# A fused cross-attention kernel: where the low half of one split is subtracted

## The reference, cut to what matters

```python
# layer 0, by sample; 8 heads of 32 channels
q, k, v = Wq @ y + bq, Wk @ y + bk, Wv @ x + bv
attn = softmax(q_h @ k_h.T / sqrt(256))            # 32 x 32 a head
o = Wo @ (attn @ v) + bo + x
x1 = groupnorm(o) * gn_w + gn_b                    # over the whole sample
# layer 1, by chunk of 64 positions
q, k, v = proj(y)                                  # W_in, b_in
p = softmax(q_h @ k_h.T / sqrt(32) + mask)         # 64 x 64 a head and chunk
z = (W_out @ (p @ v) + b_out) * mask + x1
out = (z - mean(z)) * rsqrt(var(z) + eps)          # each channel, over positions
```

## Time and profile before

| | |
|---|---|
| median of three runs | 1559.06 us |
| the profiled execution | 1557.83 us |
| its span, first to last instruction | 1556.0 us |
| TensorE (PE) busy | 1527.3 us, 98% |
| VectorE (DVE) busy | 1324.1 us, 85% |
| ScalarE (ACT) busy | 999.5 us, 64% |
| GpSimd (POOL) busy | 451.4 us, 29% |
| mean granted TensorE clock | 0.996 |
| DMA, mean | 101 GB/s |
| VectorE, low half of `y` (line 820) | 64 instructions, 77.8 us |

### The profile page before, as it was taken

How to read it: one execution, slowest core, us unless ns; L and a number is a source line. 1 busy time by engine, 2 the same in 40 slices (tenths; PEclk the granted TensorE clock), 3 DMA queues, 4 the chain that set the end, 5 groups by cost and what they waited for, 6 DMA issues and landing times.

```text
span 1556.0 us, 55525 instructions
## 1 busy us (share of the span) xinstructions
PE 1527.3 (98%) x24660; PEld 1287.2 (83%) x24660; DVE 1324.1 (85%) x2028; ACT 999.5 (64%) x1808; POOL 451.4 (29%) x294
## 2 busy tenths in 40 slices
PE   9999999999999999999999999999999999999995
PEld 7888888888888888888888888888888888888874
DVE  5778888888898888988888888888888889898897
ACT  5656665666656667566575665766666665666655
POOL 1114133141331414214142241423314133141331
PEclk9999999999999999999999999999999999999998
DMA  7132331424324242241433415234142331424221
GB/s 256 54 96 77 110 123 41 145 84 117 110 67 133 70 142 86 83 123 63 143 83 103 124 45 151 88 98 123 49 150 79 120 111 55 133 82 127 59 72 67
DMA packets 96399, 157.33 MB, mean 101 GB/s; under 512 B 5408, under 2 KB 38304, under 8 KB 96032
## 3 DMA queue, kind: packets, MB, share of 16 engines
q1 hardware_dynamic: 96160, 153.78, 32.0%
HBM read 120.20 MB, written 33.55 MB: 99 GB/s over the span
## 4 chain that ended last, share of the span: by engine, by line
PE 86%; DVE 12%; issue 1%; ACT 1%; POOL 0%; ACTq 0%; POOLq 0%; DVEq 0%
PE pj_ps L313 41%; PE l_ps L313 12%; PE l_ps L433 7%; PE s_ps L337 7%; PE w_ps L348 7%; PE w_ps L366 6%; DVE o_sb L994 3%; PE s_ps L326 2%; PE l_ps L450 2%; DVE row_sum L851 1%; DVE prob L846 1%; DVE x_lo L829 1%; DVE y_lo L820 1%; DVE u_sb L868 1%; DVE m_lo L907 1%
## 5 line engine op out<-in xcount | busy, mean ns | idle before, releaser
L1125 POOL TENSOR_TENSOR prob<-prob,row_inv 128x1024 f32<-128x1024 f32 x128 | 258.3, 2018 | 903.8 <-DVE row_inv L856 903.8
L668 ACT CAST att_hi<-w_ps 128x256 fp32r<-128x256 f32 x256 | 82.9, 376 | 227.4 <-PE w_ps L366 221.0
L313 PE MATMUL pj_ps<-y_hi,w_hi 128*128 128x512 f32 x510 | 206.8, 405 | 0.0
L313 PE MATMUL pj_ps<-y_hi,w_lo 128*128 128x512 f32 x510 | 201.3, 395 | 0.0
L313 PE MATMUL pj_ps<-y_lo,w_hi 128*128 128x512 f32 x510 | 201.2, 394 | 0.0
L851 DVE TENSOR_REDUCE row_sum<-prob 128x16 f32<-128x1024 f32 x128 | 154.9, 1210 | 52.1 <-ACT prob L650 52.1
L839 DVE TENSOR_REDUCE row_max<-s_ps 128x16 f32<-128x1024 f32 x128 | 155.9, 1218 | 33.7 <-PE s_ps L337 31.1
L645 ACT COPY prob_t<-w_ps 128x512 f32<-128x512 f32 x256 | 149.8, 586 | 14.2 <-PE w_ps L348 11.4
L1142 POOL TENSOR_TENSOR o_sb<-o_sb,u_sb 128x1024 f32<-128x1024 f32 x60 | 157.9, 2642 | 2.6 <-ACT o_sb L658 2.6
L824 DVE TENSOR_TENSOR yt_hl<-yt_raw,yt_hl 128x1024 fp32r<-128x1024 f32 x64 | 119.8, 1872 | 42.7 <-ACT yt_hl L613 40.8
L846 DVE TENSOR_TENSOR prob<-s_ps,row_max 128x1024 f32<-128x1024 f32 x128 | 155.4, 1214 | 0.1
(11 more groups left out here) (141 smaller groups left out, 3540.0 us busy)
## 6 DMA issues: line engine op xcount, KB each, us to landing
y_raw<-in_ctx SPq DMA_DIRECT2D x64, 512.0 KB, 4.8
yt_raw<-in_ctx_t SPq DMA_DIRECT2D x64, 512.0 KB, 4.8
x_raw<-in_x SPq DMA_DIRECT2D x64, 512.0 KB, 5.3
out_z<-o_sb SPq DMA_DIRECT2D x60, 512.0 KB, 3.6
mask_b<-in_mask SPq DMA_DIRECT2D x64, 256.0 KB, 4.0
out_z<-o_sb SPq DMA_DIRECT2D x8, 256.0 KB, 2.6
u_sb<-in_w SPq DMA_DIRECT2D x2, 512.0 KB, 5.8
w_sb<-in_w SPq DMA_DIRECT2D x1, 1024.0 KB, 11.1
```

Of the source, the lines that this page charges most:

```text
L313: last = mm(dst, lhs, rhs, start=i == 0, stop=i == len(todo) - 1)
L1125: nc.gpsimd.tensor_tensor(cut, cut, row_inv[:, u % 2, :].unsqueeze(2).to_broadcast([P, 2 * HEADS, CHUNK]), ALU.mult).then_inc(probs_done, 1)
```

## The change

VectorE's call of `split_y` in the loop is removed (its two calls ahead of the loop stay). GpSimd gets a function of the same name with the same wait, operands and semaphore, called in the slots with j = 2, after the slot's `scale_probs`, `group_norm` and `join`. Before its loop GpSimd waits until the two low halves made ahead of it are counted. 62 subtractions move.

```diff
@@ VectorE, body of the loop
-                    if j == 2 and not (last and b + 2 >= BLOCKS):
-                        split_y(n, b + 2)
@@ GpSimd
+            def split_y(n, b):
+                pool.wait_ge(y_hi_done, count(n, 4, b))
+                nc.gpsimd.tensor_tensor(y_lo[:, b % 2], y_raw[:, b % 2], y_hi[:, b % 2], ALU.subtract).then_inc(y_lo_done, 1)
@@ GpSimd, body of the loop
                     if not first and T_Z <= s < T_Z + BLOCKS:
                         join(n - 1, s - T_Z)
+                    if s % PAIRS == 2 and not (last and s // PAIRS + 2 >= BLOCKS):
+                        split_y(n, s // PAIRS + 2)
                     if s == T_STAT and not first:
                         instance_norm(n - 1)
 
             pool.wait_ge(power_set, 1)
+            pool.wait_ge(y_lo_done, 2)
             over_samples(pool, body)
```

## The result

The changed kernel takes 1563.66 us in the median of 13 runs (1562.61 to 1564.56), the kernel before 1559.65 in 13 runs beside it: a ratio of 1.0025, with a 95% interval of 1.0016 to 1.0033, so 2.5 to 5.1 us slower. 1565.0 was forecast. The profiled execution took 1563.65 us, its span is 1561.9.

The account below looks back on a forecast made before the run. TensorE, busy 1527.3 of 1556.0 us, was taken as the bound. A loss of 12.6 us at a_wide less 6.7 won at o_bias gives +5.9, put on the median of 1559.06: 1565.0 us, range 1556 to 1572.

Parts of the forecast that it names:

- The gain: Slots 10 and 11: with the subtraction off VectorE, TensorE's wait for o_bias goes, 14 x 0.48 = 6.7 us won.
- The length of the subtraction: GpSimd's 128x1024 subtraction takes 2.41 us, as its addition of line 1142; ends 1.91 and 3.36.
- B: Slot 10: the subtraction is shorter, nearer line 1125's 1.91 us; net -1.6 us, 1557.5 us; chance 0.10.
- C: The subtraction is much longer, through fp32r or VectorE holding GpSimd: up to +20 us, 1579 us; chance 0.06.
- The hold: Slot 10: a_wide stands until GpSimd's subtraction ends; TensorE loses 0.84 us in each of 15 samples, 12.6 us.
- Rival A: Slot 10: a_wide is not held beside GpSimd's subtraction, only the gain is left, 1552.4 us; chance 0.15.
- Rival D: Another result becomes late ahead of o_bias, no gain, 1571.7 us; or gain and loss cancel, 1559; chance 0.07.
- The other three slots: Slots 2, 6 and 14: the moved subtractions meet nothing that costs TensorE time; taken as nothing.
- no slack at `a_wide`: Slot 10: a_wide ends at 1405.51, TensorE loads line 471's weights, which need it, at 1405.57; any delay costs time.

Follow-up runs that it names:

- mask from PSUM: Changed kernel with a_wide's second input read from PSUM in place of the head mask in SBUF, the mask not applied: 1551.49 us.
- memset: Changed kernel with GpSimd's subtraction in slot 10 left out and a zero fill of 2816 columns of an unused tile in its place: 1553.85 us.
- `a_wide` early: VectorE's two a_wide instructions moved to the head of slot 10: 1551.65 us on the changed kernel, 1555.85 us on the kernel before.

## Why the prediction was right

The mechanism was the one forecast, step by step.

- *The gain.* Forecast 0.48 us a sample at `o_bias` in samples 1 to 14, read from the last sample, which lacked the subtraction by itself. Measured 0.472, with line 868 idle for 0.56 us in both.
- *The length of the subtraction.* Forecast 2.41, measured 2.395 in the median of all 62; `fp32r` as output costs GpSimd nothing beside the 2.41 of line 1142, which writes f32. Rivals B and C fall.
- *The hold.* Forecast: `a_wide` ends 0.45 behind GpSimd's end, 0.84 late. Measured 0.41 behind and 0.76 late. The 0.08 are a subtraction shorter by 0.03 (2.38 in slot 10), and 0.04 in the ending, which I had put together from one row of a pair; the rest is rounding. 15 x 0.76 = 11.4 in place of 12.6 is the term that was off: 1.2 of the 1.9 us between the forecast difference of 5.9 and the measured 4.0. The difference forecast lies outside the measured interval, 2.5 to 5.1; with the measured terms, 11.4 - 6.6 = 4.8, it lies inside. The time of 1565.0 came closer (1.3 off) by luck: the kernel before stands at 1559.65 in 13 runs, 0.6 above the three runs that the forecast was added to.
- *Rival A* (no hold, faster) falls by the trace. Its price was right all the same: the two kernels in which the subtraction's place is kept and `a_wide` isn't held stand at 1551.5 (mask from PSUM) and 1553.9 (memset), where 1552.4 was given for it.
- *Rival D* falls: nothing else became late ahead of `o_bias`.
- *The other three slots* were taken as nothing, and are nothing. In slot 6 the copy of line 921 went ahead of the queued subtraction, as assumed. The reason given for slots 2 and 14, "at most one SBUF input", was too weak in itself: line 994 has one and was held as soon as the subtraction met it. It is that no such instruction falls beside the subtraction there; line 994 is held 15 times in the kernel before and 15 times in the changed one. (By its own terms the subtraction of slot 14 ends at 1433.1 and not at 1433.0, which changes nothing.)

One thing the forecast said in passing was more right than I took it: that there was no slack at `a_wide`. It was slightly negative, 0.07 us a sample, so the most to be won at these two waits was not 6.7 us but 6.7 + 1.1, about 8 (an estimate from the table).

## What to carry to other kernels

Before work goes to an idle GpSimd, lay the new instruction's interval over VectorE's row. If the new instruction reads SBUF, look in that interval for VectorE instructions with two SBUF inputs, and for scalings and copies like those of lines 994 and 921; each of these stood here until GpSimd had finished, and what counts is who waits for it, not how busy either engine is. When the bound engine waits for one result of a busy one, first move other work behind that result on the same engine: here that gave the gain of 0.47 a sample and made no new wait. And look in the trace of before for instructions that are longer than their shortest copies: the hold of line 994 stood there in every sample but the first. A sample, block or iteration that lacks the work in question is a free experiment, already in the trace of before.

## What the runs showed of the hardware

- Issue times that are close don't tell who is held. With `a_wide` early, VectorE's first instruction is issued 0.02 us ahead of GpSimd's rescaling, and is still the one that is held: it lasts 2.07 us in place of 0.34, in all 16 samples. With VectorE 0.16 us ahead (line 829, kernel before) it is GpSimd that is held, 2.75 in place of 1.91.
- A GpSimd memset of 2816 columns, 2.45 us long, doesn't hold `a_wide`, with its two SBUF inputs, at all (0.60 for the pair).
- GpSimd's subtraction takes 1.29, 1.84 and 2.38 us for 512, 768 and 1024 columns: some 0.2 us and 2.13 ns a column. Its rescaling, whose second input is one number for 64 elements, takes 1.90 for 1024.
